# Message weights from a PSUM bank, key compares without a mask, and segment sums that cross a tile finished at the tiles

## What is computed

```python
# L1_gnn (a1, m1): softmax over each target's edges; dst is sorted
ex    = exp(alpha - segment_max(alpha, dst)[dst])
alpha = ex / segment_sum(ex, dst)[dst]
out   = segment_sum(v_j * alpha[:, :, None], dst) + x @ Ws + bs
# L2_gnn (fl, m2): filtered messages, summed by the edge's row
filt  = silu(rbf @ Wf1 + bf1) @ Wf2 + bf2
agg   = segment_sum(x[col] * filt, row)
# L3_gnn (a3, m3): as L1, and every node also has an edge to itself (loops)
src, dst = concatenate([src, loops]), concatenate([dst, loops])
e     = leaky_relu(a_src[src] + a_dst[dst], 0.2)
out   = segment_sum(xh[src] * softmax_over_dst(e), dst) + bias
```

## Time and profile before

| | |
|---|---|
| time, median of 3 runs | 4857.91 us (4852.75 to 4869.78) |
| the profiled execution, its own time | 4873.99 us |
| its span | 4872.2 us, 75057 instructions |
| mean granted TensorE clock | 0.857 |
| TensorE (PE) busy | 3686.5 us, 76% |
| weight loads (PEld) | 2955.3 us, 61% |
| VectorE (DVE) | 2915.4 us, 60% |
| GpSimd (POOL) | 2586.5 us, 53% |
| ScalarE (ACT) | 1667.2 us, 34% |
| DMA, mean over the span | 160 GB/s |
| DMA, busiest of 40 slices | 336 GB/s |

### The profile page before, as it was taken

How to read it: one execution, slowest core, us unless ns; L and a number is a source line. 1 busy time by engine, 2 the same in 40 slices (tenths; PEclk the granted TensorE clock), 3 DMA queues, 4 the chain that set the end, 5 groups by cost and what they waited for, 6 DMA issues and landing times. The chain is left out here.

```text
span 4872.2 us, 75057 instructions
## 1 busy us (share of the span) xinstructions
PE 3686.5 (76%) x20734; PEld 2955.3 (61%) x20786; DVE 2915.4 (60%) x5941; ACT 1667.2 (34%) x3757; POOL 2586.5 (53%) x2597
## 2 busy tenths in 40 slices
PE   7786489869999997135089999279999577777188
PEld 6664367758777785133078888257777466665165
DVE  7788374558988896521278888333333645554653
ACT  5563222013333332001066666133333223333032
POOL 0075767667777773675677777500000277775400
PEclk9986689989999998556599999689999878887579
DMA  5065456489999996333278887310000167666300
GB/s 78 1 211 174 144 186 198 167 267 329 333 330 329 332 336 189 100 88 111 64 198 237 233 229 227 107 62 1 0 0 0 51 179 200 197 197 179 95 14 26
DMA packets 642022, 779.41 MB, mean 160 GB/s; under 512 B 149190, under 2 KB 562361, under 8 KB 638106
## 3 DMA queue, kind: packets, MB, share of 16 engines
q0 software_dynamic: 120624, 316.61, 21.2%
q1 hardware_dynamic: 350852, 284.27, 20.7%
q10 hardware_dynamic: 170374, 176.38, 11.7%
HBM read 509.08 MB, written 272.20 MB: 160 GB/s over the span
## 5 line engine op out<-in xcount | busy, mean ns | idle before, releaser
L2606 POOL DMA_INDIRECT fl_far<-x_table,fl_index x416 | 481.7, 1158 | 144.1 <-issue 126.4
L2340 POOL DMA_INDIRECT a_far<-src_table,a_index x416 | 450.7, 1083 | 132.1 <-issue 124.0
L1450 POOL DMA_INDIRECT by_dst<-dst_row,place x416 | 414.7, 997 | 191.4 <-issue 102.4
L2019 POOL DMA_INDIRECT a_far<-kv_table,a_index x416 | 434.8, 1045 | 145.5 <-issue 113.1
L2643 PE MATMUL ps<-fl_w,fl_hid 128*128 128x256 f32 x1664 | 405.0, 387 | 38.8 <-ACT ps L2715 37.3
L3311 POOL DMA_INDIRECT starts<-p_near,p_at x25 | 24.4, 975 | 708.2 <-DMA starts<-p_zero 693.1
L2053 PE MATMUL ps<-a_w,a_edge_t 128*128 128x256 f32 x1664 | 395.3, 381 | 0.0
L2643 PEld LDWEIGHTS ps<-fl_w,fl_hid 128*128 128x128 f32 x1664 | 312.4, 192 | 88.8 <-issue 48.9
L2053 PEld LDWEIGHTS ps<-a_w,a_edge_t 128*128 128x128 f32 x1664 | 301.1, 191 | 32.6
L1078 ACT ACTIVATE f_hid<-ps,f_bn 128x320 f32<-128x320 f32 x320 | 197.6, 617 | 327.7 <-PE ps L1032 327.7
L1119 DVE SCALAR_TENSOR_TENSOR x_sb<-ps,f_cw,x_sb 128x256 f32 x200 | 96.8, 484 | 343.9 <-PE ps L1043 343.9
(11 more groups left out here) (536 smaller groups left out, 9338.9 us busy)
## 6 DMA issues: line engine op xcount, KB each, us to landing
partial<-a_out ACTq DMA_DIRECT2D x208, 546.0 KB, 4.4
a_edge<-by_dst SPq DMA_DIRECT2D x104, 516.0 KB
partial_f<-fl_out ACTq DMA_DIRECT2D x26, 2056.0 KB, 10.2
dst_row<-in_edge_attr SPq DMA_DIRECT2D x52, 1024.0 KB, 6.1
xn_sb<-q_table SPq DMA_DIRECT2D x416, 128.0 KB
fl_keys<-key_rows SPq DMA_DIRECT2D x26, 1024.0 KB, 5.3
a_keys<-local_rows SPq DMA_DIRECT2D x104, 128.0 KB
xt<-partial SPq DMA_DIRECT2D x14, 512.0 KB, 4.8
```

The costliest lines, as they stand in the source:

```text
L1450: self.nc.gpsimd.indirect_dma_start(out=self.table, out_offset=bass.IndirectOffsetOnAxis(ap=self.place[:, n:n + 1], axis=0), in_=self.row[ ...
L2019: gathered[b % 4].count(nc.gpsimd.indirect_dma_start(out=far[:, b, u, :], out_offset=None, in_=kv_table, in_offset=bass.IndirectOffsetOnAx ...
L2340: gathered[b].count(nc.gpsimd.indirect_dma_start(out=far[:, b, u, :], out_offset=None, in_=src_table, in_offset=bass.IndirectOffsetOnAxis( ...
L2606: gathered[q * 4 + t // 4].count(nc.gpsimd.indirect_dma_start(out=far[:, q, t, :], out_offset=None, in_=table, in_offset=bass.IndirectOffs ...
```

## The change

Four parts.

1. **a3.** Once a chunk the weights are copied from `weight` into the fourth quarter of PSUM bank 0 (`WEIGHTS`), and the message multiply reads them there. It now stands ahead of the two scans in a chunk's first quarter.
2. **Filter.** `same` is a plain compare with the row's key, without the mask. Each row of a tile then holds the tile's whole sum of its node, the first row too.
3. **Merges.** The nodes are split. A node inside one tile has its sum in its own row: `take_own` (for m3 `weigh_own`) ends it there, with a mask `keep`. For a node that crosses, the sum is finished at the tile in which it ends, once for all 416 tiles: SP loads, beside the last rows, the first row of each next tile (`opening`), the key column of `by_dst` or `by_src` (`key`) and the key of the row behind the next tile (`opening_after`). `find_places` works out where each finished row belongs: the node's row, or past the table if the node doesn't end in the next tile. `weigh_tiles` and `merge_tiles` bring carried sum and opening row together on 104 x 4 rows. GpSimd scatters them with four indirect DMAs (`send`) to `finals`, which is the first half of `kv_table`; SP loads all of it back with five plain loads (`far`), and `add_far` adds them where a node crosses (`spans`), 25 multiply-adds. The carry table, its store and the 25 far gathers are gone. The sends stand behind 20 own gathers in m1 and m2 and behind all 25 in m3. In m3 eight more gathers, the self rows of the tiles (`tile_value`, `tile_score`), stand ahead of the own gathers.
4. **Side job in m1.** `Share.begin` issues its first two loads ahead of SP's wait for the sends.

```diff
+    def begin(self, sp):
+
+        if self.first == self.rows.looped and not self.begun:
+            for k in range(self.rows.RING):
+                self.rows.load(sp, self.first + k)
+        self.begun = True
...
+        SCORES, NODES, TOPS, WEIGHTS = (ps[:, 0, k * P:(k + 1) * P] for k in range(4))
...
+                    if sums and s % 4 == 0:
+                        dve.wait_ge(weighed, i * 2 + (b - MSG) // 4 + 1)
+                        ch.link(nc.vector.tensor_copy(WEIGHTS, weight[:, s // 4].rearrange("p t h -> p (t h)")))
                     if c is not None:
                         dve.wait_ge(node_copied, c + 1)
+                    if sums:
+                        if not isinstance(i, int) or m >= 2:
+
+                            dve.wait_ge(summed, m * 2 - 2)
+                        w = WEIGHTS.rearrange("p (t h) -> p t h", h=HEADS)[:, (s % 4) * 4:(s % 4) * 4 + 4, :]
+                        nc.vector.tensor_tensor(heads(msg[:, s % 2, :, 0:D]), heads(far[:, s, :, 0:D]), w.unsqueeze(3).broadcast_to([P, 4, HEADS, HD]), ALU.mult).then_inc(msg_ready, 1)
+                    if c is not None:
...
-                            nc.vector.scalar_tensor_tensor(same[:, qb % 2 * 4 + u, :], keys[:, q, b * 4 + u, :], edge[:, q, b * 4 + u, NG:NG + 1],
-                                                           core.c("le"), ALU.is_equal, ALU.mult).then_inc(same_made, 1)
+                            nc.vector.tensor_scalar(same[:, qb % 2 * 4 + u, :], keys[:, q, b * 4 + u, :], edge[:, q, b * 4 + u, NG:NG + 1], None,
+                                                    ALU.is_equal).then_inc(same_made, 1)
...
+        SENT_AFTER = TILES if self_rows is not None else TILES - GROUP
...
+                def load_ahead(to, tiles, column, sem):
+                    first, three = tiles * P, 3 * QT * P
+                    sp.dma_start(to[:, 0:3], partial[first:first + three, column].rearrange("(q p r) w -> p q r w", q=3, r=P)[:, :, 0, :],
+                                 allow_slow_non_contiguous=True).then_inc(sem, 16)
+                    sp.dma_start(to[0:QT - tiles, 3], partial[first + three:EPAD, column].rearrange("(p r) w -> p r w", r=P)[:, 0, :],
+                                 allow_slow_non_contiguous=True).then_inc(sem, 16)
+                sp.dma_start(part[:], of_tile(partial, P - 1)).then_inc(loaded, 16)
+                sp.dma_start(key[:], of_tile(by_key[:, key_at:key_at + 1], P - 1), allow_slow_non_contiguous=True).then_inc(key_loaded, 16)
+                sp.wait_ge(blanked, 1)
+                load_ahead(opening, 1, slice(0, W + 1), opening_loaded)
+                load_ahead(opening_after, 2, slice(W, W + 1), after_loaded)
...
-                sp.dma_start(carry.rearrange("(q p) w -> p q w", q=4), out[:]).then_inc(stored, 16)
+                if share is not None:
+                    share.begin(sp)
+                sent.wait(sp, 4 * 16)
+                for g in range(GROUPS):
+                    sp.dma_start(far[:, g * GROUP:(g + 1) * GROUP, :], finals[g * GTOK:(g + 1) * GTOK, :].rearrange("(a p) d -> p a d", p=P)).then_inc(far_loaded[g], 16)
...
+                def send():
+                    pool.wait_ge(done, 1)
+                    for q in range(4):
+                        sent.count(nc.gpsimd.indirect_dma_start(out=finals, out_offset=bass.IndirectOffsetOnAxis(ap=at[:, q:q + 1], axis=0),
+                                                                in_=merged[:, q, :], in_offset=None,
+                                                                bounds_check=NPAD - 1, oob_is_err=False))
+
+                if self_rows is not None:
+                    pool.wait_ge(placed, 1)
+                    for q in range(4):
+                        gather(tile_self, tile_value[:, q, :], self_rows[0], key_i[:, q:q + 1])
+                        gather(tile_self, tile_score[:, q, :], self_rows[1], key_i[:, q:q + 1])
                 pool.wait_ge(indexed, 1)
                 for a in range(TILES):
-                    gather(own_gathered, own, a, partial, end_i)
-                pool.wait_ge(stored, 16)
-                for a in range(TILES):
-                    gather(far_gathered[a // GROUP], far, a, carry, carry_i)
+                    if a == SENT_AFTER:
+                        send()
+                    gather(own_gathered[a // GROUP], own[:, a, :], partial, end_i[:, a:a + 1])
+                if SENT_AFTER == TILES:
+                    send()
...
+                def find_places():
+                    dve.wait_ge(key_loaded, 16)
+                    dve.wait_ge(opening_loaded, 32)
+                    dve.wait_ge(after_loaded, 32)
+                    ch.add(nc.vector.tensor_tensor(goes_on[:, 0], opening[:, :, W], last_node[:], ALU.is_equal))
+                    ch.add(nc.vector.tensor_tensor(goes_on[:, 1], opening_after[:, :, 0], last_node[:], ALU.is_equal))
+                    ch.settle()
+                    ch.link(nc.vector.tensor_tensor(goes_on[:, 0], goes_on[:, 1], goes_on[:, 0], ALU.subtract))
+                    ch.link(nc.vector.tensor_scalar(goes_on[:, 0], goes_on[:, 0], 1.0, float(NPAD), ALU.add, ALU.mult))
+                    ch.add(nc.vector.tensor_tensor(at[:], goes_on[:, 0], key[:, :, 0], ALU.add))
...
+                        ch.add(nc.vector.tensor_tensor(by_head(merged[:]), by_head(before[:, :, 0:D]), widen(e[:, 2]), ALU.mult))
+                        values = by_head(opening[:, :, 0:D])
+                        ch.add(nc.vector.tensor_tensor(values, values, widen(e[:, 1]), ALU.mult))
+                        if self_rows is not None:
+                            values = by_head(tile_value[:, :, 0:D])
+                            ch.add(nc.vector.tensor_tensor(values, values, widen(e[:, 3]), ALU.mult))
+                        ch.settle()
+                        ch.link(nc.vector.tensor_tensor(merged[:], merged[:], opening[:, :, 0:D], ALU.add))
+                        if self_rows is not None:
+                            ch.link(nc.vector.tensor_tensor(merged[:], merged[:], tile_value[:, :, 0:D], ALU.add))
+                    else:
+                        dve.wait_ge(summed, 1)
+                        ch.link(nc.vector.tensor_tensor(merged[:], before, opening[:, :, 0:D], ALU.add))
                     dve.sem_inc(done, 1)
...
+                def take_own(g):
+                    T = slice(g * GROUP, (g + 1) * GROUP)
+                    own_gathered[g].wait(dve, GROUP * 16)
+                    if self_rows is not None:
+                        weigh_own(g, T)
+                    elif tops:
+                        ch.link(nc.vector.reciprocal(f[:, 0, T], own[:, T, D:sums]))
+                        ch.link(nc.vector.tensor_tensor(f[:, 0, T], f[:, 0, T], bh(keep[:, T]), ALU.mult))
+                        v = by_head(own[:, T, 0:D])
+                        ch.link(nc.vector.tensor_tensor(v, v, widen(f[:, 0, T]), ALU.mult))
+                        ch.add(nc.vector.tensor_tensor(x[:, T, :], x[:, T, :], own[:, T, 0:D], ALU.add))
                     else:
-                        ch.link(nc.vector.tensor_tensor(agg[:, T, :], own[:, T, 0:D], bias_sb[:].unsqueeze(1).broadcast_to([P, GROUP, D]), ALU.add))
+                        ch.add(nc.vector.tensor_tensor(agg[:, T, :], own[:, T, 0:D], keep[:, T].unsqueeze(2).broadcast_to([P, GROUP, D]), ALU.mult))
...
+                    take_own(0)
+                merge_tiles()
+                to = x if agg is None else agg
+                def add_far(g):
+                    dve.wait_ge(far_loaded[g], 16)
+                    for a in range(g * GROUP, (g + 1) * GROUP):
+                        ch.add(nc.vector.scalar_tensor_tensor(to[:, a, :], far[:, a, :], spans[:, a:a + 1], to[:, a, :], ALU.mult, ALU.add))
+                for g in range(1 if self_rows is not None else 0, GROUPS - 1):
+                    take_own(g)
+                if self_rows is not None:
+                    take_own(GROUPS - 1)
+                ch.settle()
+                for g in range(GROUPS - 1):
+                    add_far(g)
+                if self_rows is None:
+                    take_own(GROUPS - 1)
+                ch.settle()
+                add_far(GROUPS - 1)
...
+            finals = kv_table.rearrange("n w -> (n w)")[0:NPAD * D].rearrange("(n d) -> n d", d=D)
```

More of the change, by code:

```diff
@@ L2510, in _ @@
                     take_index(0, b)
[L2511 removed]
+                run(dve, MSG, quarter, lambda: ch.loop(BODIES - 2, 2 * (1 + 4 + 2 + 1)))
 def filter_stage(core, name, edge_rows, key_rows, table, wf1, bf1, wf2, bf2, partial):
@@ L2873, in merge_stage @@
         ident = core.c("ident")
+        key_at = by_key.shape[1] - 2
         with st.block() as block:
```

207 lines of the change are left out of this document (105 added, 102 removed).

## The result

The changed kernel takes 4748.86 us (median of 4 runs, 4746.25 to 4753.91) against 4855.69 us of the kernel before (a fourth run has joined the three of the table above; 4852.75 to 4869.78): ratio 0.9775, 95% interval 0.9753 to 0.9798. The profiled execution took 4746.25 us, its span is 4744.4 us.

The account below looks back on a forecast made before the run. GpSimd was taken to set the pace in a3, the filter and m1, the last far rows to end m2, VectorE to decide m3. The terms summed to -118 us, giving 4740 us against the median, range 4708 to 4786.

Parts of the forecast that it names:

- a3, -31: In a3: weights read from a bank end nearly all the gather stretch beside the message multiply; -31 us, bounds -34 and 0.
- Filter, -15: In the filter: the shorter compare shifts where gathers meet subtractions, easing GpSimd's stretch; -15 us, floor -38, ceiling +8.
- m1, -30: In m1: GpSimd has 45 issues in place of 66 and starts about 1 us earlier; -30 us, bounds -22 and -34.
- m2, -26: In m2: finished rows return in five plain loads, done at 3128 against 3154.52; -26 us, bounds -20 and -29.
- m3, -17: In m3: VectorE's groups take 9.1 us in place of 12.5, though the first starts later; -17 us, bounds -10 and -20.
- Ends and the rest, +1: At the ends of stages: eleven more semaphores cleared per merge; +1 us together, bounds 0 and +2.
- A: In the filter: the new compare holds the port as the subtraction does, so the -15 goes; 4772 us, chance 0.10.
- B: In a3: traffic, not the operand, stretches gathers, so -31 becomes 0; 4771 us, chance 0.05.
- C: In the merges: the chain from sums through sends to load back ends each; saving 52, not 73; 4761 us, chance 0.15.
- D: In the filter: the stage runs up to TensorE, -38 in place of -15; 4717 us, chance 0.15.
- E: In a3: denser quarters get TensorE's lower clock level throughout, so messages come late; +163 us, 4934 us, chance 0.02.

Follow-up runs that it names:

- the second pair: Changed kernel and kernel before, both unedited, profiled again side by side on one more chip: changed 4736.88 us, ratio 0.9782; before against itself 0.9994.

## Why the prediction was right, and where it was not

Predicted were 4740 us and -118; measured 4748.86, inside the stated 4708 to 4786, and -107. Four of the five stage terms came out to 2 us in both pairs of profiles, one of them by luck; the fifth, the filter's, was wrong.

- **a3, -31.** Right in mechanism and size, by two errors that cancel. No stretch was left at all (-34.7 and -36.5), and the tail paid 5 to 6 us in place of 1. The rows came later, and TensorE's granted clock fell to its lower level 6 us behind the last gather, after TensorE had stood 2.8 us, and stayed there for 14 us; before the change it was down for 7 us around the last gather.
- **Filter, -15.** This is the step that failed. "Now gathers and the VectorE sequence are locked in a bad phase" was true of one execution. With the mask restored the time is the same, and in the second pair the stage differs by 3 us. The price should have been about -3. The error was made twice over: the profiled execution lay 16 us over the median, with 30 us more in this stretch than the second profile has, and the sum took 15 us off for it and then was set against the median.
- **m1, -30.** -28.5 and -29.5. The sends were reached 31.0 us into the stage (28 at least was said) and waited for nothing; what was not priced is that the sends and the first three gathers behind them take 1.2 to 1.8 us each beside the wide multiplies and adds.
- **m2, -26.** -24.8 and -25.0. It ended on the loads, as said.
- **m3, -17.** -16.7 twice. First group at 26 us after the start (24.5 said), 8.8 us a group (9.1), no wait for the finished rows, 1.2 us for the self rows.
- **Ends and the rest, +1.** The prediction had no row for it. From a merge's last work to the next stage it is 0.6 us more in m2, 0.9 more in m3 and 0.7 less in m1, +0.8 together, inside the pieces of the merges. The pieces that the change leaves alone came to -1.6 and -1.4 us.

Without the filter the terms sum to -103; the same pieces measured -103 and -103 in the two pairs. The medians differ by 107 us in both sets of runs, which leaves about 4 for the filter. Of the rivals, A did not come (a gather that begins inside a new compare gains 0.02 us on average, 0.08 at most), nor B, C and D. E's mechanism showed in a3's tail alone.

## What to carry to other kernels

Where GpSimd issues gathers at full pace, look at every VectorE instruction beside it with both inputs in SBUF: it can hold a gather for nearly its own time, and a row of short ones without gaps can hold one for longer. Putting one operand into a bank removes this, if nobody needs the bank; cutting the instruction shortened it in the filter. Before a stretch is priced that depends on how two engines fall into step, profile the kernel a second time, and don't set a saving from an execution above the median against the median.

## What was not expected

- The kind of instruction made no difference between the two that were tried: 2.02 us for a gather beside a scalar_tensor_tensor of 1.22 us.
- A row of short instructions without gaps can hold a scatter for longer than any one of them: 5.24 us beside multiply-adds that start every 0.40 us. Two scatters beside the same row took 1.26 and 1.25 us; what sets them apart is open.
- A stage whose gathers run freely can be slower: 596 us at 1.008 us a gather against 575 at 1.072.
- Three sets of runs have 4844 to 4860 us for the kernel before, a fourth, on another chip, 6022. The stages compared here are slower only where they loop; no reason for the gaps in them shows in the trace.
